# Second layer of the old pair ahead of the first layer of the new one, norm turned later, gate turn ahead of the carry turn, bias over 128 rows

## The reference

```
x = x + gnn(layernorm(x));  x = x + ffn(layernorm(x))
gnn: ft = feat @ W (4 heads of 64);  e = leaky(e_src[src] + e_dst[dst], 0.2)
     a = softmax of e over the edges of one dst, times dist
     out[dst] += ft[src] * a
ffn: w = softmax(mean(x) @ Wr + br) over 8 experts (the mean is over a batch of one)
     h = relu(bn1(x @ W1[e] + b1));  h = relu(bn2(h @ W2[e] + b2))
     y = h @ Wo[e] + bo[e];  out = sum over e of w[e] * y
```

## Time and profile before

| what | value |
|---|---|
| median of 3 runs | 1558.78 us (1555.95 to 1559.75) |
| profiled execution, first to last instruction | 1556.4 us |
| PE busy | 1485.0 us (95%) |
| PEld busy | 1298.3 us (83%) |
| DVE busy | 1231.7 us (79%) |
| POOL busy | 1063.0 us (68%) |
| ACT busy | 742.2 us (48%) |

### The profile page before, as it was taken

The page is one execution under the profiler, slowest core; times in us unless marked ns, Lnnn a source line. Parts: engine busy times, 40 slices in busy tenths (PEclk is TensorE's granted clock), DMA queues, the critical chain, the costliest instruction groups (busy, mean ns, idle before and its releaser), DMA issues.

```text
span 1556.4 us, 24165 instructions
## 1 busy us (share of the span) xinstructions
PE 1485.0 (95%) x8478; PEld 1298.3 (83%) x8478; DVE 1231.7 (79%) x2302; ACT 742.2 (48%) x1293; POOL 1063.0 (68%) x951
## 2 busy tenths in 40 slices
PE   6928999999999999999999999999999999999998
PEld 4727888878888888888888888888888888888887
DVE  7746787887788888878888888888888888888751
ACT  3500444444455555545555555554555555555543
POOL 4176767777778777777777877777777787787000
PEclk9959999999999999999999999999999999999999
DMA  8776344353543444353344444434334444443000
GB/s 239 203 233 192 110 137 124 106 141 94 144 121 111 122 126 127 103 142 108 103 135 118 112 119 118 128 106 137 108 107 134 119 111 119 129 111 91 18 7 8
DMA packets 106070, 187.50 MB, mean 120 GB/s; under 512 B 38357, under 2 KB 70490, under 8 KB 105919
## 3 DMA queue, kind: packets, MB, share of 16 engines
q0 software_dynamic: 44688, 123.13, 28.5%
q1 hardware_dynamic: 60701, 62.29, 13.9%
q10 hardware_dynamic: 560, 0.52, 0.1%
HBM read 172.72 MB, written 14.42 MB: 120 GB/s over the span
## 4 chain that ended last, share of the span: by engine, by line
PE 82%; DVE 9%; DMA 3%; issue 2%; ACT 2%; POOL 1%; SPq 0%; DVEq 0%; ACTq 0%
PE bankH L831 39%; PE bankY L860 21%; PE bankE L783 5%; PE bankE L784 5%; PE bankB L761 3%; PE bankE L776 2%; DVE gath L1431 1%; POOL gath L675 1%; DVE msg_lo L1437 1%; ACT h L1030 1%; DMA table<-gath 1%; PE bankA L808 1%; DVE x L1506 1%; DMA gath<-table,src_win 1%; PE bankA L799 1%
## 5 line engine op out<-in xcount | busy, mean ns | idle before, releaser
L675 POOL DMA_INDIRECT gath<-table,src_win x900 | 1042.5, 1158 | 336.0 <-issue 245.2
L1030 ACT ACTIVATE h<-bankH,bn_shift,bn_scale 128x250 f32<-128x250 f32 x800 | 400.9, 552 | 314.9 <-PE bankH L831 314.7
L831 PE MATMUL bankH<-h,w 128*128 128x250 f32 x1600 | 380.5, 380 | 2.8 <-ACT h L1030 2.1
L860 PE MATMUL bankY<-wo,h 128*125 128x256 f32 x1600 | 378.4, 379 | 1.1 <-DVE x L1506 1.1
L831 PE MATMUL bankH<-xT,w 128*128 128x250 f32 x1600 | 370.9, 374 | 0.3 <-ACT h L1030 0.3
L860 PEld LDWEIGHTS bankY<-wo,h 128*125 128x125 f32 x1600 | 296.1, 187 | 43.2 <-issue 1.4
L831 PEld LDWEIGHTS bankH<-h,w 128*128 128x128 f32 x1600 | 295.6, 191 | 43.4 <-issue 9.6
L831 PEld LDWEIGHTS bankH<-xT,w 128*128 128x128 f32 x1600 | 296.7, 190 | 32.2 <-ACT h L1030 0.4
L1437 DVE TENSOR_TENSOR msg_lo<-gath,msg_hi 128x2340 fp32r<-128x2340 f32 x90 | 234.3, 2603 | 88.0 <-ACT msg_hi L1002 88.0
L1002 ACT ACTIVATE msg_hi<-gath 128x2340 fp32r<-128x2340 f32 x90 | 193.8, 2154 | 217.0 <-PE bankE L784 192.0
L1506 DVE SCALAR_TENSOR_TENSOR x<-bankY,gate,x 125x256 f32<-125x256 f32 x400 | 173.9, 476 | 116.7 <-PE bankY L860 116.1
(11 more groups left out here) (190 smaller groups left out, 1027.6 us busy)
## 6 DMA issues: line engine op xcount, KB each, us to landing
onehot_t<-dst_low SPq DMA_DIRECT2D x48, 576.0 KB, 5.9
gath<-table,src_win POOLq DMA_INDIRECT x900, 2.9
x_res<-in_x SPq DMA_DIRECT2D x25, 250.0 KB
out<-x SPq DMA_DIRECT2D x25, 250.0 KB
table<-gath SPq DMA_DIRECT2D x25, 227.5 KB
w<-in_L_ffn_W SPq DMA_DIRECT2D x8, 512.0 KB
gath<-in_x SPq DMA_DIRECT2D x5, 672.0 KB
wo<-in_L_ffn_Wo SPq DMA_DIRECT2D x4, 512.0 KB
```

Of the source, the lines that this page charges most:

```text
L675: pool.indirect_dma_start(gath[:, g.slot(u), t, :], None, table, bass.IndirectOffsetOnAxis(src_win[:, g.win, u, t:t + 1], 0)).then_inc(row ...
L831: mm = pe.matmul(target[:, hc * 2 * NT:(hc + 1) * 2 * NT], weights[:, e * KC + c, hc * P:(hc + 1) * P], operand(c), start=(c == 0), stop=( ...
L860: mm = pe.matmul(bankY[0:NT, u * D:(u + 1) * D], h2[:, e % 2, c, u, :], wo[:, e * KC + c, :], start=(c == 0), stop=(c == KC - 1))
L1030: ins = act.activation(target[:, e % 2, hc, :, :].rearrange("p u n -> p (u n)"), source[:, hc * 2 * NT:(hc + 1) * 2 * NT], ACT.Relu, bias= ...
```

## The change

PE and ACT take the second layer of expert 7 of the old pair (and its relu) at the start of step 0, ahead of the first layer of the new pair. `turn_x1` moves behind the third layer of step 7. Both roots of the norm stand behind `relu2` of their step. `turn_gate` stands ahead of `turn_carry`. `gate_t` and `bo_rows` get 128 rows, the last 96 of them zero (two memsets at the start), and the bias product runs over all 128. DVE's loop, SP and POOL are unchanged.

```diff
--- before.py
+++ after.py
@@ -221,7 +221,7 @@
         wo = sb("wo", [P, EX * KC, D])
         wr = sb("wr", [P, KC, EX])
         br_all = sb("br_all", [P, EX])
-        bo_rows = sb("bo_rows", [4 * EX, D], F32R)
+        bo_rows = sb("bo_rows", [P, D], F32R)
         bo_pick = sb("bo_pick", [4 * EX, 2])
         bn_scale = sb("bn_scale", [P, 2, EX * KC])
         bn_shift = sb("bn_shift", [P, 2, EX * KC])
@@ -267,7 +267,7 @@
         rsum = sb("rsum", [P, 2])
         rinv = sb("rinv", [P, 2])
         gate = sb("gate", [P, RING, 2, EX])
-        gate_t = sb("gate_t", [4 * EX, 2, NT], F32R)
+        gate_t = sb("gate_t", [P, 2, NT], F32R)
         gate_parts = sb("gate_parts", [P, 2, 4, EX], F32R)
         h1 = sb("h1", [P, 2, KC, 2, NT])
         h2 = sb("h2", [P, 2, KC, 2, NT])
@@ -878,6 +878,8 @@
 
                 for s in range(EX + 1):
                     run = f is not None and s < EX
+                    if run and s == 0 and not f.begins(1):
+                        layer2(f + -1, EX - 1, nothing)
                     if run:
                         layer1(f, s, nothing)
                         if s == 0:
@@ -894,15 +896,13 @@
                         turn_bounds(f, a)
                         for _ in small:
                             pass
-                    if run and (s >= 1 or not f.begins(1)):
-                        layer2(*before(f, s, 1), nothing)
+                    if run and s >= 1:
+                        layer2(f, s - 1, nothing)
+                    if run and s == 1:
+                        turn_gate(f)
                     if plan is STEADY:
                         for k, tiles in plan.ends(s):
                             turn_carry(g, k)
-                    if run and s == 1:
-                        turn_gate(f)
-                    if g is not None and s == plan.turn:
-                        turn_x1(g)
                     if run and (s >= 2 or not f.begins(1)):
                         layer3(*before(f, s, 2), nothing)
                     if g is not None:
@@ -910,6 +910,8 @@
                             aggregate(g, c)
                             if c % 2:
                                 stay_busy(g, 8 if c < 2 else 14)
+                    if g is not None and s == plan.turn:
+                        turn_x1(g)
                     if plan is not STEADY:
                         for k, tiles in plan.begins(s):
                             turn_runs(g, k)
@@ -1021,7 +1023,7 @@
 
             def keep_gate(f):
                 act.wait_ge(gateT_done, f.n + 1)
-                act.activation(gate_t[:].rearrange("e u n -> e (u n)"), bankA[0:4 * EX, 256:256 + 2 * NT], ACT.Copy).then_inc(gateT_kept, 1)
+                act.activation(gate_t[0:4 * EX].rearrange("e u n -> e (u n)"), bankA[0:4 * EX, 256:256 + 2 * NT], ACT.Copy).then_inc(gateT_kept, 1)
 
             def relu(f, e, l, done, target, source):
                 act.wait_ge(done, f.n * EX + e + 1)
@@ -1052,22 +1054,21 @@
                 plan = plan_of(g)
                 for s in range(EX + 1):
                     run = f is not None and s < EX
+                    if run and s == 0 and not f.begins(1):
+                        relu2(f + -1, EX - 1)
                     if run:
                         relu1(f, s)
                     if run and s == 0:
                         exp_route(f)
                     if a is not None and s == plan.bounds:
                         keep_bounds(a)
+                    if run and s >= 1:
+                        relu2(f, s - 1)
                     if g is not None and s == max(plan.residuals):
                         root1(g, 0)
-                        if f is None:
-                            root1(g, 1)
+                        root1(g, 1)
                     if g is not None and s == plan.turn:
                         keep_x1T(g)
-                    if run and (s >= 1 or not f.begins(1)):
-                        relu2(*before(f, s, 1))
-                    if f is not None and g is not None and s == max(plan.residuals):
-                        root1(g, 1)
                     if run and s == 1:
                         keep_gate(f)
                     for k, tiles in plan.ends(s):
@@ -1097,6 +1098,8 @@
             own.did(dve.tensor_copy(base[:], base_i[:]))
             own.did(dve.tensor_copy(node[:], node_i[:]))
             own.did(dve.tensor_copy(bound[:], bound_i[:]))
+            own.did(dve.memset(gate_t[:].bitcast(F32), 0.0))
+            own.did(dve.memset(bo_rows[:].bitcast(F32), 0.0))
             own.did(dve.memset(logit[:], -BIG))
             own.did(dve.memset(reset[:], -BIG))
             own.did(dve.memset(row_reset[:], -BIG))
@@ -1211,7 +1214,7 @@
                     own.settle()
                     own.did(dve.tensor_scalar(bo_low, bo_low, bo_pick[:, 0:1], None, ALU.mult))
                     own.settle()
-                    dve.scalar_tensor_tensor(bo_rows[:], bo_high.bitcast(F32), bo_pick[:, 1:2], bo_low, ALU.mult, ALU.add).then_inc(bo_ready, 1)
+                    dve.scalar_tensor_tensor(bo_rows[0:4 * EX, :], bo_high.bitcast(F32), bo_pick[:, 1:2], bo_low, ALU.mult, ALU.add).then_inc(bo_ready, 1)
                 if n == 19:
                     dve.wait_ge(p_flag, 1)
                     own.did(dve.tensor_copy(plan_f[:, 0:J], bankH2[0:1, 0:J]))
```

## The result

The changed kernel takes 1569.06 us (median of 4 runs, 1568.64 to 1569.27), the kernel before on the same chip 1558.52 (4 runs, 1555.95 to 1559.75): a ratio of 1.0068 with a 95% interval of 1.0054 to 1.0082. It is slower, by 10.5 us where 10.0 were forecast. The profiled spans are 1567.2 and 1556.4.

A forecast was written before the change was run, and what follows sets the result against it. PE was taken to bound the kernel, with 82% of the chain of waits. Steady stages +6.5, early pairs +3.6, last pair -0.4, memsets +0.3: +10.0 on 1558.8 gives 1568.8 us; own range 1564 to 1573, with rivals 1557 to 1577.

The forecast's parts named there:

- start, up to the first turn of the norm: Kernel start: two memsets on DVE cost a few tenths, +0.3 us (0 to 0.6).
- pairs 2 and 3: Turn of the runs later by 0.9 us in pair 2, 1.69 in pair 3; the bias returns 0.38 in each.
- pair 4: Turn of the runs at step 0's end comes 1.69 us later; a later wait swallows the bias's 0.38.
- steady stages: Aggregating pairs 6 to 24, 19 stages: 0.62 lost less 0.28 gained, +0.34 us each, +6.5 in all.
- end: Last pair: takes only the gain of the wider bias, -0.4 us.
- the early pairs: Pairs 2, 3 and 4: runs turned at step 0's end come later, +3.6 us in all (0 to +4.5).
- Step 7: Old pair's last step: moved roots let expert 6's second layer start on time, 3.78 to 3.38 us; moved turn needs no wait.
- the copy: ACT's copy of the turn of the norm: hidden by expert 7's second layer now, by expert 5's third layer before.
- The chain behind A(0)'s end: Step 0, new pair's first layer through ACT and DVE to the turn of the runs: 5.31 us, PE waits 1.02.
- The table load: ACT, step 0: stays directly behind the first layer's relu, ahead of exp; 1.55 us from load to rsum.
- The drain: ACT, behind the table load: the skill's about 1.38 us would lengthen step 1's wait by some 1.4; the forecast left it out.
- Steps 1 and 2: Gate ahead of carry +0.10 us, bias over 128 rows -0.38; together -0.28, from 8.18 to 7.90.

The follow-up runs named there:

- the second experiment: Changed kernel with the second layer of expert 7 and its relu put back behind the new pair's first layer: 1570.59 us, ratio 1.0070.
- the early table, the third experiment: Changed kernel plus a spare one-column exp on ACT at step 0, ahead of the relu of expert 7's second layer: 1555.28 us, ratio 0.9972.
- the first experiment: Kernel before with only the second layer of expert 7 and its relu moved ahead of the new pair's first layer: 1586.41 us, ratio 1.0167.
- the keep-busy experiment: Changed kernel plus nine spare matmuls on PE ahead of the turn of the runs in step 0 of pairs 2, 3 and 4: 1566.6 us, ratio 1.0047.

## Why the prediction was right, step by step

The forecast's mechanism held, and its time (1568.8 against 1569.06). The terms, in the two profiled executions (the last but one group of the third layer starts at 1556.83 and at 1546.01, 10.8 apart; pairs are cut at the start of A(7), and the last steady stage ends with A(0) of the last pair):

| term | predicted | in the traces |
|---|---|---|
| start, up to the first turn of the norm | +0.3 | +1.87 |
| pair 1 | 0 | +0.1 |
| pairs 2 and 3 | +1.8 (0.9 + 1.69, less 0.38 twice) | +5.5, of it 3.3 the clock |
| pair 4 | +1.7 | +1.6 |
| pair 5 | 0 | -0.3 |
| steady stages | +6.5 (19 of 0.34) | +2.4 (19 of 0.13) |
| end | -0.4 | -0.4 |

The forecast's terms add to 9.9; its +3.6 for the early pairs is 0.1 more than its own parts give.

- **Step 7.** Right to the hundredth in the stage shown: 3.38 for A(7) and B(6), the turn without a wait, A(0)'s end 1.31 later on average (1.29 predicted). What the prediction said of the copy (hidden by B(7)) was right, and the second experiment shows that it is needed.
- **The chain behind A(0)'s end.** Right in its links, mis-sized by 0.20 in its sum: 5.11 instead of 5.31 on average. In the stage shown the relu starts 0.26 behind A(0)'s end, the load 1.03 later, rsum 1.54 later, all as forecast; from rsum to the turn of the runs it is 2.33 and not the 2.47 taken from the earlier trace rows. The two copies of the logits take 0.41 together, where they took 0.55 before; why they do is not settled. From rsum's start to that of the last scan it is 1.91 in nearly every stage before and with the early table, 1.72 to 1.82 in the changed kernel and 1.72 in the first experiment. So PE waits 0.82 on average (0.87 in the stage shown), not 1.02, and the steady pair pays 0.13, not 0.34. That is the largest error of the sum, 4.1 us: the net of +1.31, -0.87 (5.98 to 5.11) and -0.29 is small beside its terms, and more than half of it goes when one of them is off by 0.20. The value for rsum to turn should have had a range of its own.
- **The table load.** That it stays where it is, behind A(0)'s relu, and is paid in full, is shown by the third experiment, which takes it away. The drain that the Trainium skill states ("ScalarE: Activation LUTs", section "What ACT_TABLE_LOAD costs") is not there: exp starts at 796.83, 0.01 behind the load's end (795.54 + 1.28). With it the wait of 0.87 would have been about 2.3, as an estimate from that page's figure.
- **Steps 1 and 2.** Right: 8.18 to 7.89 against 7.90 forecast, of it -0.38 the bias (alone: -0.38) and +0.08 the swap (alone: +0.08; +0.10 forecast). The split within the bias's part is another than forecast: its two matmuls still start 0.42 ahead of B(1), not 0.24, but they start 1.51 behind A(2), not 1.69. Why is open; the sum of 1.93 is the forecast's.
- **The early pairs.** The delay of the turn of the runs came as forecast in pairs 2 and 3 (about 0.9 and 1.7) and the bias gives 0.38 back there. Not foreseen was the clock: PE's idle time ahead of the later turn went from 1.26 to 2.15 us in pair 2, and the clock fell in two of three such places. That is 3.3 of the 5.5 us, and the keep-busy experiment shows it. The prediction read the waits as lost time only, and did not ask what an idle stretch does to the clock, though both kernels hold spare matmuls for the first pair (`stay_busy`, in the diff above). Pair 4 takes from 62.0 to 66.9 us, step 3 to step 3, in the traces of kernels without the change or with one part of it, so its +1.6 is not worth much.
- **The start.** The +1.9 is not the memsets. The first turn of the norm stands at 150.8 to 154.8 us in nine kernels with them (mean 152.9) and at 151.3 to 154.5 in four without (mean 152.7). The difference of the means, 0.2, is near the forecast of 0.3, but the scatter is far larger than either.

So the sum was right partly by luck: 4.1 us too much in the steady stages, against 3.3 of clock that was missing and 1.6 of scatter at the start of one trace. What the scatter is in the medians, which are 10.5 apart and not 10.8, stays open; so does why the clock falls behind one such stretch and not behind another.

## What to carry to other kernels

When a group on the bounding engine is moved ahead of another, follow not only what the moved one gains but which chain hangs on the end of the one it passes; here 1.3 us of delay met a chain through ACT and DVE with no slack. Look for a table load at the head of such a chain: a spare activation of the same table, put where ACT is idle, took it off the path, some 14 us in all here (3.3 of them the clock of the early pairs), and then the next waiting item (a mask in DVE's order) could be moved too. Edits that look separate can be two halves of one (roots and turn, turn and B(7)); time them both alone and together.

## What the hardware showed that was not expected

- A group of few rows in the contraction costs about 0.1 us to enter or to leave, in the groups next to it: C(7) lasts 1.99 behind a turn of 8 rows and 1.89 behind one of 125; a bias of 32 rows starts 1.78 behind A(2) and makes the next B last 1.96, with 128 rows (96 of them zero) it is only 1.93 from A(2)'s start to B's, where it was 2.20, and B lasts 1.85. Together 0.38 us per group of two matmuls, 6 to 7 us over the kernel. Few rows are not the only such case: C(6) lasts 1.97 behind the route, which has 128 rows and 8 columns. For the bias an experiment changed the rows alone; for the turn of 8 rows the swap shows only where the 0.1 falls. The Trainium skill, "TensorE: Matmul & The Clock Gate", section "Why this matters for your kernels", has a single matmul of 32 rows take as long as one of 128. From the bias's start to B's it is indeed 0.42 with either number of rows; but the whole from A(2)'s start to B's end is 0.38 longer with 32, so that sentence alone gives the wrong price for a small group among large ones.
- Idle stretches of PE of 2.15 to 2.21 us ahead of the turn of the runs, three in the changed kernel and three with B(7) moved alone, were followed by a granted clock of 0.52 to 0.54 in four places and of 1.00 in two. In the other runs this stretch was 1.65 us or shorter in pairs 2, 3 and 4, and A(1) took 1.79 behind every one of them. Spare matmuls in the changed kernel's stretches kept A(1) at 1.79 in all three pairs.
